# Seven instead of five down products per tile in short passes, with one more buffer each for their h, and router steps one block later

## The reference, cut to what matters

```python
x = x + layernorm(attention(layernorm(x)))      # x: 16 x 256 x 128, 16 heads of 8
x = x + layernorm(ffn(layernorm(x)))

def ffn(x):                                     # 4096 tokens, width 128
    combine = router(x)                         # 4 of 8 groups, 6 of 32 experts, weights scaled by 2.5
    h = relu(einsum('th,eih->tei', x, up_w)) ** 2 * combine[:, :, None]   # 32 experts, 64 wide
    moe = einsum('tei,ehi->th', h, down_w)
    shared = relu(x @ shared_up_w.T) ** 2 @ shared_down_w.T               # 256 wide
    return moe + shared
```

## Time and profile before

| | |
|---|---|
| median of 3 runs | 527.96 us (527.72 to 528.67) |
| the profiled execution | 530.13 us, of which the span from first to last instruction is 528.3 us |
| TensorE busy | 473.9 us (90%) |
| VectorE, ScalarE, GpSimd busy | 405.1, 373.0, 228.1 us (77%, 71%, 43%) |
| attention | 0 to about 276 us |
| feed-forward, 8 tiles | about 276 to 521 us, then the last norm and the store |
| chain that ended last | PE 60%, DVE 11%, issue 8%, SP's queue 6%, ACT 6%, POOL 5% |
| granted TensorE clock | mean 0.954; at 1.2 GHz from 26.1 to 67.1 us and from 265.1 to 268.5 us, at 2.4 GHz otherwise |

### The profile page before, as it was taken

The page is one execution under the profiler, slowest core; times in us unless marked ns, Lnnn a source line. Parts: engine busy times, 40 slices in busy tenths (PEclk is TensorE's granted clock), DMA queues, the critical chain, the costliest instruction groups (busy, mean ns, idle before and its releaser), DMA issues.

```text
span 528.3 us, 11035 instructions
## 1 busy us (share of the span) xinstructions
PE 473.9 (90%) x3416; PEld 274.2 (52%) x3416; DVE 405.1 (77%) x1063; ACT 373.0 (71%) x739; POOL 228.1 (43%) x544
## 2 busy tenths in 40 slices
PE   2458999999999999978799899999999999999994
PEld 1213454544444454544346566666666666766662
DVE  4688788899999989978827769597786859587453
ACT  2415788887988988877676567868777777857552
POOL 6054332225434635221103545829385674716241
PEclk9555899999999999999899999999999999999998
DMA  6443434444444443330024244536254644525441
GB/s 196 133 135 107 126 121 128 125 132 134 124 129 143 141 124 105 109 104 31 4 86 153 87 164 127 197 89 211 85 153 151 179 166 124 190 98 196 135 126 40
DMA packets 51737, 67.48 MB, mean 128 GB/s; under 512 B 4192, under 2 KB 35168, under 8 KB 51680
## 3 DMA queue, kind: packets, MB, share of 16 engines
q1 hardware_dynamic: 51680, 66.78, 40.1%
HBM read 51.17 MB, written 15.20 MB: 126 GB/s over the span
## 4 chain that ended last, share of the span: by engine, by line
PE 60%; DVE 11%; issue 8%; SPq 6%; ACT 6%; POOL 5%; DMA 3%; POOLq 0%; DVEq 0%; ACTq 0%
PE pY L1383 8%; PE pS L1383 7%; PE pO L1302 6%; PE pS L1246 6%; PE pS L1367 6%; PE pS L1369 6%; PE pS L1368 5%; DVE mneg L921 4%; SPq L408 3%; PE pS L1252 2%; ACT probs L701 2%; SPq L396 2%; DMA k_scratch<-k_parts 2%; PE pX L1231 1%; DVE r L1090 1%
## 5 line engine op out<-in xcount | busy, mean ns | idle before, releaser
L921 DVE TENSOR_REDUCE mneg<-pS 128x2 f32<-128x512 f32 x256 | 164.2, 686 | 23.4 <-PE pS L1246 22.6
L701 ACT ACTIVATE probs<-pS 128x512 f32<-128x512 f32 x256 | 144.3, 596 | 25.5 <-PE pS L1252 23.8
L1246 PE MATMUL pS<-kp,qp 48*128 48x256 bf16 x512 | 87.3, 290 | 20.9 <-DVE mneg L921 9.6
L787 ACT ACTIVATE h_ring<-r 128x512 f32<-128x512 f32 x104 | 65.1, 628 | 45.7 <-DVE r L1090 24.6
L1367 PE MATMUL pS<-qp,up_hi 128*128 128x512 f32 x144 | 88.5, 615 | 0.0
L1252 PE MATMUL pS<-qp,kp 51*128 51x256 bf16 x512 | 87.5, 281 | 0.9 <-ACT probs L701 0.7
L1302 PE MATMUL pO<-probs,vv 128*32 128x256 f32 x1024 | 73.6, 394 | 0.4 <-ACT oT_sb L653 0.4
L1246 PEld LDWEIGHTS pS<-kp,qp 48*128 48x128 bf16 x512 | 34.1, 96 | 70.9 <-DVE mneg L921 42.1
L1090 DVE SCALAR_TENSOR_TENSOR r<-pS,probs 128x512 f32<-128x512 f32 x64 | 43.8, 685 | 21.9 <-PE pS L1369 19.0
L1090 DVE SCALAR_TENSOR_TENSOR r<-pS,c_ring 128x512 f32<-128x512 f32 x64 | 43.9, 688 | 17.7 <-PE pS L1369 15.9
L1369 PE MATMUL pS<-qp,up_lo 128*128 128x512 f32 x144 | 56.8, 394 | 0.0
(11 more groups left out here) (193 smaller groups left out, 853.4 us busy)
## 6 DMA issues: line engine op xcount, KB each, us to landing
c_ring<-c_scratch SPq DMA_DIRECT2D x32, 512.0 KB, 4.0
probs<-c_scratch SPq DMA_DIRECT2D x32, 512.0 KB, 3.9
qp<-q_scratch SPq DMA_DIRECT2D x64, 96.0 KB
kp<-k_scratch SPq DMA_DIRECT2D x64, 96.0 KB
q_scratch<-q_parts SPq DMA_DIRECT2D x16, 192.0 KB, 2.4
k_scratch<-k_parts SPq DMA_DIRECT2D x16, 192.0 KB, 2.6
q_scratch<-q_parts SPq DMA_DIRECT2D x16, 128.0 KB, 2.4
k_scratch<-k_parts SPq DMA_DIRECT2D x16, 128.0 KB, 2.3
```

The source lines that it names most:

```text
L701: nc.scalar.activation(probs[j][:, hh], pS2[n % S2_RING][:, :, :], ACT.Exp, scale=SCALE).then_inc(exp_done, 1)
L787: nc.scalar.activation(h_ring[:, (n - at) % HRING], r_sb[n % URING][:, :], ACT.Square).then_inc(sq_done, 1)
L921: nc.vector.tensor_reduce(mneg[u % 2][:, :, hh, k], pS1[n % S1_RING][:, :].rearrange("p (a s) -> p a s", a=TH), AX.X, ALU.max, negate=True ...
L1246: return mm(pS1[n % S1_RING][:, T * th:T * (th + 1)], qp[slot][rows, k, P * th:P * (th + 1)], kp[slot][rows, k, :], start=True, stop=True)
```

## The change

SPLIT has seven blocks instead of five, every second routed block from 2 to 14, so seven of the 18 down products of a tile are in the short form and eleven in the whole form. h_hi and h_whole get four buffers, h_lo three. Room for them comes from q_rest and k_rest, which become one tile that is also x_cut, and from c_ring: only its first buffer stays its own, the second is now in probs 5; groups 1, 2 and 3 of tile 0 all wait for pv_done. The router steps in tiles from 1 on stand one block later. GpSimd's order in the tiles gets two more lows and is rearranged; in attention norm_x moves ahead of part2 and part3.

```diff
@@ -65,8 +65,8 @@
 SBLK = SI // P
 FBLK = RBLK + SBLK
 HRING, URING = 3, 4
-SPLIT = (2, 5, 8, 11, 14)
-SPLIT_LAG, HI_RING, LO_RING = 6, 3, 2
+SPLIT = (2, 4, 6, 8, 10, 12, 14)
+SPLIT_LAG, HI_RING, LO_RING = 6, 4, 3
 CGROUP, CRING = 2, 4
 NGROUP = RBLK // CGROUP
 ROOT_SCALE = ROUTED_SCALE ** 0.5
@@ -75,7 +75,7 @@
 
 
 ROUTE_AT = ((3, 4, 5, 6, 7, 8, 9, 11),
-            (0, 1, 2, 3, 4, 5, 6, 8))
+            (1, 2, 3, 4, 5, 6, 7, 9))
 SPREAD_AT = (13, 11)
 NORM_Y_AT = ((3, 4, 5, 6), (1, 3, 4, 5))
 NORM_X1_AT = ((12, 13, 14, 15), (11, 12, 13, 14))
@@ -159,7 +159,8 @@
         xnT = [sb(f"xnT{i}", [P, T]) for i in range(3)]
         q_parts = [sb(f"q_parts{i}", [P, 3, T], BF16) for i in range(2)]
         k_parts = [sb(f"k_parts{i}", [P, 3, T], BF16) for i in range(2)]
-        q_rest, k_rest = sb("q_rest", [P, T]), sb("k_rest", [P, T])
+        qk_rest = sb("qk_rest", [P, 2 * T])
+        q_rest, k_rest = qk_rest[:, 0:T], qk_rest[:, T:2 * T]
 
         qp = [sb(f"qp{i}", [P, UB, T], BF16) for i in range(RING)]
         kp = [sb(f"kp{i}", [P, UB, T], BF16) for i in range(RING)]
@@ -180,7 +181,8 @@
 
         x_hi, x_lo = ([ring[XSLOT + i][:, :, :].rearrange("p a b -> p (a b)").bitcast(F32R) for i in range(2)]
                       for ring in (qp, kp))
-        x_cut = sb("x_cut", [P, TILE])
+        assert TILE == 2 * T
+        x_cut = qk_rest
         e_sb = sb("e_sb", [P, C4, E])
         score, choice = sb("score", [P, C4, E]), sb("choice", [P, C4, E])
         pair_hi, pair_lo = sb("pair_hi", [P, C4 * GROUPS, 2]), sb("pair_lo", [P, C4 * GROUPS, 2])
@@ -195,20 +197,21 @@
         root_v, root_h = (sb(n, [P, C4, E]) for n in ("root_v", "root_h"))
         root_t = comb
         cT = sb("cT", [E, TILE])
-        c_ring = ([sb(f"c_ring{i}", [P, CGROUP, TILE]) for i in range(2)]
+        c_ring = ([sb("c_ring0", [P, CGROUP, TILE])]
                   + [probs[i][:, :, :, :].rearrange("p a b c -> p (a b c)").rearrange("p (k t) -> p k t", k=CGROUP)
-                     for i in range(2)])
+                     for i in (5, 0, 1)])
         r_sb = [sb(f"r{i}", [P, TILE]) for i in range(URING)]
         h_ring = sb("h_ring", [P, HRING + 1, TILE])
-        spare = probs[4][:, :, :, :].rearrange("p a b c -> p (a b c)")
-        h_whole = [h_ring[:, HRING], spare[:, 0:TILE], spare[:, TILE:2 * TILE]]
+        spare = [probs[i][:, :, :, :].rearrange("p a b c -> p (a b c)")[:, TILE * n:TILE * (n + 1)]
+                 for i, n in ((3, 1), (4, 0), (4, 1))]
+        h_whole = [h_ring[:, HRING]] + spare
         h_hi, h_lo = ([sb(f"{name}{i}", [P, TILE], F32R)[:, :] for i in range(n)]
                       for name, n in (("h_hi", HI_RING), ("h_lo", LO_RING)))
         down_hi, down_lo = (sb(f"down_{n}", [P, len(SPLIT), D], F32R) for n in ("hi", "lo"))
-        down_whole = down_sb[:, :, :].rearrange("p (a b) d -> p a b d", b=3)[:, 0:len(SPLIT), 0]
+        down_whole = down_sb[:, :, :].rearrange("p (a b) d -> p a b d", b=2)[:, 0:len(SPLIT), 0]
         fT_sb = sb("fT_sb", [P, TILE])
 
-        assert all(k - SBLK == 3 * s for s, k in enumerate(SPLIT))
+        assert all(k - SBLK == 2 * s for s, k in enumerate(SPLIT))
         assert (HRING + 1) * TILE == RBLK * P and TILE >= SI
         up_in = [h_ring[:, i] for i in range(NCUT - 1)] + [fT_sb[:, 0:SI]]
         w_cut = r_sb[0]
@@ -463,7 +466,7 @@
                 n = NGROUP * i + g
                 if g == 0:
                     sp.wait_ge(c_written, 16 * (i + 1))
-                if n in (2, 3):
+                if n in (1, 2, 3):
                     sp.wait_ge(pv_done, 4 * NB)
                 if n >= CRING:
                     ti, tg = divmod(n - CRING, NGROUP)
@@ -604,11 +607,11 @@
                     part3(nc.gpsimd, pool.wait_ge, 2)
                     chain_x(1, FIRST, NT)
                 if u % 2 == 0 and u >= 2:
+                    if u // 2 + 3 < NB:
+                        norm_x(u // 2 + 3)
                     if u // 2 + 2 < NB:
                         part2(u // 2 + 2)
                         part3(nc.gpsimd, pool.wait_ge, u // 2 + 2)
-                    if u // 2 + 3 < NB:
-                        norm_x(u // 2 + 3)
 
                 for i in range(2):
                     if u == 2 * PREP[i] + 3:
@@ -621,21 +624,24 @@
             chain_y(2)
             for i in range(NTILE):
                 low(i, 0)
+                low(i, 1)
                 if i + 2 < NTILE:
                     residual1(i + 2)
                 if i == 0:
-                    low(i, 1)
+                    low(i, 2)
+                    low(i, 3)
                 if i + 1 < NTILE:
                     root_of_sum(i + 1)
                 if i >= 1:
-                    low(i, 1)
+                    low(i, 2)
                 if i + 2 < NTILE:
                     chain_x1(i + 2)
-                low(i, 2)
                 if i >= 1:
+                    low(i, 3)
                     chain_f(i - 1)
-                low(i, 3)
                 low(i, 4)
+                low(i, 5)
+                low(i, 6)
                 if i + 3 < NTILE:
                     chain_y(i + 3)
                 if i >= 1:
@@ -778,7 +784,7 @@
                     nc.scalar.activation(h_hi[at % HI_RING], r_sb[n % URING][:, :], ACT.Square).then_inc(hi_done, 1)
                     if at >= HI_RING:
                         act.wait_ge(lo_done, at - HI_RING + 1)
-                    elif at == 1:
+                    elif at in (1, 2, 3):
                         act.wait_ge(pv_done, 4 * NB)
                     nc.scalar.activation(h_whole[at % HI_RING], r_sb[n % URING][:, :], ACT.Square).then_inc(sq_done, 1)
                     return
```

## The result

The changed kernel takes 536.75 us (median of 4, 535.64 to 537.65) against 528.32 (4 runs, 527.72 to 530.92) for the kernel before beside it: a ratio of 1.0139, 95% interval 1.0106 to 1.0172. The forecast was 525.9 with a range to 529.8, so both the sign and the range were wrong. The profiled execution took 537.65 us (span 535.9) where that of before took 530.13 (span 528.3). The kernel before was run again beside each of the three sets of experiments and took 529.2, 529.3 and 530.25 us there, so experiments are compared by their ratios to it; one execution of the first experiment was of a slower kind, and the ratio leaves it out.

What follows compares the result with a forecast made beforehand. TensorE was taken to set the pace; -2.7 - 2.1 + 4.6 + 0.7 - 2.6 = -2.1 took the profiled 530.13 to 528.0, or a median of 525.9 us (0.4% less), range 521.0 to 529.8.

Steps and rivals of the forecast that it cites:

- Passes, -2.7: Second-stage down products on TensorE: each converted product saves 0.17 us, two more per tile in 8 tiles, 2.7 us.
- The wait at block 6: Tiles 1 to 6: TensorE's wait of 0.35 us before block 6's down product goes, saving 2.1 us.
- GpSimd's queue in tiles 1 to 5, +4.6: w_root starts at 416.7, its chain ends at 428.25, and TensorE waits 0.9 us per tile in block 16.
- Rival 2: Tiles: step 4 waits 1.3 us behind block 4's low, rect 7 at 416.2; +3.5 us, 529.4 in all; chance 0.2.
- the schedule without a meeting (415.1): Tile 4, VectorE: rect 7's start at 415.1, before adding step 5's products meeting residual1, which made it 415.5.
- the point of 415.5: Tile 4: latest start of block 7's rect, 415.5 or so, before TensorE waits for its product in block 10.
- my 30.27: Tiles 1 to 5: the forecast's own tile period in us, 30.06 - 0.34 - 0.35 + 0.9.
- Tile 0, +0.7: Tile 0: waits of 2.5 us go, one of some 3.2 for block 9's product comes; 0.7 lost, bounds -1.5 and +1.5.
- Attention, -2.6: Attention: norm_x moved forward removes all eight TensorE waits for xn, 2.6 of 3.0 us; bounds 0 and 3.0.
- Rival 3: Attention gives nothing because SP, issuing 18 transfers a block, becomes late: +0.5 us, 528.4 in all; chance 0.1.
- Tiles 6 and 7: Last two tiles: no wait for h_lo, tile 6 at 29.6 us; forecast for the stretch -1.03 us.
- The edits costed at nothing: Tile 0's group loads waiting for pv_done, split_down's seven slices, shared qk_rest and x_cut, extra buffers: no cost.

Runs made afterwards that it cites:

- the first experiment: Kernel before with one edit, in attention GpSimd does norm_x ahead of part2 and part3: 529.51 us, ratio 0.9984.
- short lows: GpSimd's subtractions (low) cut to 32 of 512 columns: in the changed kernel 522.74 us, ratio 0.9886; in the kernel before 525.01 us, ratio 0.9911.
- low first: Changed kernel with the low of block 6 ahead of w_root in GpSimd's order, tiles from 1 on: 530.89 us, ratio 1.0040.
- COPY replaced: Changed kernel with the two small COPYs (g_best, e_best) written as tensor_reduce over an axis of length one: 530.93 us, ratio 1.0042.
- the SP edit: SP issues attention's late load ahead of load_unit(2b+6); against the kernel before: alone 527.65 us, ratio 0.9966; with norm_x in front 524.06 us, ratio 0.9903.

## Why the prediction was wrong, step by step

**Passes, -2.7: right.** 0.17 per product, by the pair with short lows.

**The wait at block 6: right that it goes, half its size.** It was read off as 0.35; a tile without it is 0.70 shorter. Every listed wait whose tile could be run without it cost more than it says. (In rows 2 to 4 the tile without it is that of the changed kernel with short lows, which differs in more than the wait.)

| wait | listed | length with | without | price |
|---|---|---|---|---|
| square of block 6, before | 0.35 | 30.06 | 29.36 | 0.70 |
| square of block 7, low first | 0.62 | 29.93 | 29.02 | 0.91 |
| h_lo, COPY replaced | 1.02 | 30.32 | 29.02 | 1.30 |
| both, changed kernel | 0.60 + 1.29 | 31.46 | 29.02 | 2.44 |
| xn, attention block | 0.37 | 13.98 | 13.42 | 0.56 |

The list counts from the modelled end of the matmul before. A short pass is shown as 0.40 while passes start 0.23 apart, which hides 0.17 of each wait, and the first pass after a wait takes 0.34 to the next start (433.61, then 433.95), another 0.11. For block 6 the up block before the wait was also 0.12 late. This error had both signs in my sum (0.35 too little for what went, 0.4 too little for the h_lo wait, 1.30 with the COPY replaced against 0.9) and nearly cancelled.

**GpSimd's queue in tiles 1 to 5, +4.6: the mechanism right, one meeting missed, and this is the step that failed in the tiles.** The schedule can be checked event by event. Block 0's up passes start at 399.80 before and at 404.09 after, so after's times less 4.29 are on the clock that I used.

| event | forecast | after, less 4.29 |
|---|---|---|
| step 0 starts | 404.56 | 404.44 |
| rect 2 starts | 405.8 | 405.82 |
| low of block 2 starts | 407.8 | 407.83 |
| rect 4 starts (step 2 waited for that low) | 409.4 | 409.43 |
| step 4, one product | 412.15 | 412.16 |
| low of block 4 starts | 412.2 | 412.22 |
| residual1 starts | 413.8 | 413.56 |
| rect 7 starts | 415.5 | 416.22 |
| w_root starts | 416.7 | 417.38 |

VectorE and GpSimd in tile 4 of the changed kernel:

```profile
412.58 0.87 DVE L1004 TENSOR_TENSOR g_mid<-g_mid,g_low 128x32 f32<-128x32 f32 x1
...
416.45 0.28 DVE L1013 TENSOR_TENSOR masked<-choice,picked_g 128x128 f32<-128x128 f32 x1
...
417.87 1.30 DVE L980 COPY e_best<-top 128x24 f32<-128x24 f32 x1
...
419.98 0.29 DVE L1020 SCALAR_TENSOR_TENSOR comb<-e_left,score 128x128 f32<-128x128 f32 x1
...
420.51 0.69 DVE L1096 SCALAR_TENSOR_TENSOR r<-pS,probs 128x512 f32<-128x512 f32 x1
```
```profile
412.12 1.28 POOL L598 TENSOR_TENSOR h_lo<-h_ring,h_hi 128x512 fp32r<-128x512 f32 x1 [3.12 <-ACT h_ring L789]
416.51 1.37 POOL L598 TENSOR_TENSOR h_lo<-probs,h_hi 128x512 fp32r<-128x512 f32 x1 [3.11 <-ACT h_hi L784]
417.85 1.28 POOL L568 TENSOR_TENSOR xbig<-xbig,yn 128x512 f32<-128x512 f32 x1
421.67 1.02 POOL L562 TENSOR_TENSOR w_root<-w_sum,power 128x4 f32<-128x4 f32 x1 [2.55 <-DVE w_sum L1030]
...
432.29 1.27 POOL L598 TENSOR_TENSOR h_lo<-h_ring,h_hi 128x512 fp32r<-128x512 f32 x1
```

All is within 0.12 until residual1. Rival 2's dead heat was won by VectorE (416.45 against 416.51), so its step 4 took 0.28; rival 2 did not happen in tiles 1 to 5. The step that failed is the next one: I let residual1 meet the two products of step 5, at a cost of 0.4, and priced the COPY of e_best ahead of them at its short form. Residual1 came 0.24 earlier than I had it (my 413.8 didn't follow from my own numbers: a low from 412.2 for 1.29 ends at 413.5), the COPY started 0.02 behind it and took 1.30. That is 1.13 on top of the schedule without a meeting (415.1), and 416.22 is what came. The COPY's long form stood in my own rows, for g_best. Which of the two is first is itself a dead heat, and in tile 1 of the same profile it went the other way:

```profile
324.70 0.18 DVE L980 COPY e_best<-top 128x24 f32<-128x24 f32 x1
...
324.75 1.29 POOL L568 TENSOR_TENSOR xbig<-xbig,yn 128x512 f32<-128x512 f32 x1
```

The COPY started 0.05 ahead, took 0.18, block 7's product did not wait, and the tile took 30.32. In tiles 2 to 5 it started 0.02 to 0.03 behind, took 1.28 to 1.30, and the tiles took 31.26 to 31.53.

Two things follow. Rect 7 passed the point of 415.5 that I had named, and block 7's product waited: 0.91 per tile. And w_root started 0.7 later than forecast, so the price of the h_lo wait became 1.53 (31.46 less the 29.93 without it) where 0.9 stood. Per tile: -0.34 - 0.70 + 0.91 + 1.53 = +1.40, which is 31.46 less 30.06. Rival 2 had the same start of rect 7 (416.2) by another meeting, and took the later wait as unchanged; it is not, since w_root moves with rect 7. For the COPY the run with tensor_reduce shows this directly, and for the h_lo wait the run with the low in front.

With the COPY replaced the tile took 30.32 against my 30.27, and that agreement is in part luck. On the same clock (this run's times less 2.02), w_root starts at 416.36, 0.34 earlier than forecast, and the product L1020 takes 0.41 instead of 0.29, so step 5 lost 0.1 on the port where I had 0.4. The chain behind w_root took 11.76 instead of 11.56. The wait still came to 1.30, because the passes were wanted at 426.87 (430.19 less 1.30 and 2.02) and not at 427.33: of this 0.46, 0.35 is the wait at block 6, worth 0.70 and not 0.35.

The Trainium skill (SBUF — State Buffer, Who interferes with whom) states the exclusive lock that the prediction quoted. These rows agree, for a COPY of 24 columns (1.30) and a product of 128 (1.38) alike, while the tensor_reduce of 16 columns took 0.17 with a low running since 0.05 us.

**Tile 0, +0.7 less 0.34 of passes: sign right, too small by 1.3.** The two meetings came as worked out: a two-input operation of step 1 took 1.16 (287.61, behind the low of 287.42) and one of step 5 took 1.35 (298.10, behind the low of 298.01). The wait for block 9's product came too, at 2.08 (301.08) where I had 3.2, but waits for o_sb, onT and xn (0.46, 1.00, 0.69) came as well, of which I had none. With short lows the tile takes 29.03 in the changed kernel and 28.94 in the one before, so GpSimd's time carries this loss too. Which meeting makes which wait was not tried.

**Attention, -2.6: the step failed, by 4.8 us.** All eight waits for xn went, as forecast, but the time did not: in place of 2.6 us less, the eleven blocks took 2.2 more. Rival 3 had the mechanism, at a chance of 0.1, and priced it at no gain; neither the sum nor a rival had a loss there. I had looked for what else was busy on VectorE and ScalarE, and not at SP, though the issues stood in the trace with their times. SP issues for 13.1 us in a block of 14, and TensorE would need 13.42 once xn is out of the way: that should have told that xn was not the only limit.

**Tiles 6 and 7.** They gave back 0.3 instead of 1.03: tile 6 has a wait of 0.31 for block 7's square and one of 0.23 for nothing that the profile names. In tile 6, where there is no residual1, rival 2's meeting did happen: the low of block 4 started at 479.12, and step 4's product (L1013) at 479.28 took 1.26 instead of 0.28.

**The edits costed at nothing** stayed so as far as the trace tells: no wait for the group loads of tile 0 and none for split_down.

## What to carry to other kernels

When work is added to an engine that shares a port with another, lay both engines' instructions on one clock and price each small copy or two-input operation in both its short and its long form: an error of 0.24 us in one start turned 0.17 into 1.30, and two waits of TensorE hung on that. Where two starts lie within 0.1 us of each other, forecast both orders: both came up here, in one and the same run. Before a wait is taken away, measure for how long every queue issues and idles in one round of the loop, and not only the engines' busy shares; where two limits lie within a few per cent, edits that do nothing alone pay together (3.4 us here). And price a listed wait of TensorE by a period with it and a period without it.

## What the runs showed that I had not expected

The waits of TensorE that could be priced cost 0.19 to 0.35 us more than is listed; for the short passes and for block 7's product the modelled ends account for it. A max-reduction over one element copies 16 columns in 0.17 us while GpSimd's subtraction runs, where a COPY takes 1.28: that exchange together with the SP edit and norm_x gave 519.93 us, 1.7% less than the kernel before. It is not known what the changed kernel would give with GpSimd's lows placed so that nothing meets them; the tile of 29.02 with short lows bounds it, 0.34 below the best tile that was run with all of its work.
